# Three-term latent scores in row halves, expert weights addressed by a register, and four of twelve key tiles summed on GpSimd

## The chip, the cores and the metric

The kernel runs on one core of a Trainium2 chip. The metric is the device time of one execution in microseconds (us), as the median of several. The engines of the core are TensorE (PE; its weight loads are PEld), VectorE (DVE), ScalarE (ACT), GpSimd (POOL) and SyncE (SP), which here only issues DMAs. Each engine works through its own queue in order and waits at its head for semaphores that the others raise.

## The reference, cut to what matters

A decoder of two layers on 32 sequences of 56 tokens and 256 channels, each layer with self-attention, cross-attention to a context and a mixture of experts. The change touches the cross-attention of layer 0 and both mixtures. The cross-attention, after its weights are folded into one latent query of 64 numbers per head, is this (B = 32 batches, 16 heads, 56 queries, 1500 keys of 64 numbers):

```python
kv_rope = kv_c * cos[None] + _rotate_half(kv_c) * sin[None]
q_r = jnp.einsum('bshq,hqr->bhsr', q_big, W_qr)
k_r = jnp.einsum('bld,hdr->bhlr', kv_rope, W_kr)
scores = jnp.einsum('bhsr,bhlr->bhsl', q_r, k_r)
attn = jax.nn.softmax(scores, axis=-1)
ctx_c = jnp.einsum('bhsl,bld->bhsd', attn, kv_rope)
```

The mixtures send each token to two experts (of 16 in layer 0, of 7 in layer 1), and add a shared expert:

```python
for e in range(E):
    out = out + combine[:, e:e + 1] * (jax.nn.silu(xf @ w1[e]) @ w2[e])      # layer 0
u = jnp.einsum('nh,ehi->eni', xt, Wup) + bup[:, None, :]                      # layer 1
g = jax.nn.silu(jnp.einsum('eni,eij->enj', u, Wgate) + bgate[:, None, :]) * u
eo = jnp.einsum('enj,ejh->enh', g, Wdown) + bdown[:, None, :]
```

## The kernel before

It is written engine by engine: every stage is a block with one program for each engine, and semaphores order them. The latent cross-attention runs over the 32 batches, two to a turn of a hardware loop (`over_tiles`). `par` is the parity of the batch and picks one of two buffers. The 1500 keys of a batch are KT = 12 tiles of KP = 125 keys. Per batch:

- SP loads the context rows (`raw`), and copies the queries with their two halves of partitions exchanged (`QS`).
- GpSimd rotates the rows: cosine product (L1517), two sine products (L1519, L1522), their sum (L1525), and, when ScalarE has made the f16 high part of the rotated keys (`high`, L1659), the low part (L1531). Keys and queries are pairs of f16 numbers, high and low.
- TensorE transposes high and low parts of a key tile together (`turn`, L1562), eight tiles, then four, each group after the pair of tiles that `TURNS = (5, 9)` names; ScalarE evicts them to `kT` (`evacuate`, L1650).
- TensorE makes the scores of a tile for two groups of eight heads: `QT` (L1606) and then `QS` (L1610) against the same `kT`, which gives all four products of high and low parts. Two tiles make a pair; between pairs it multiplies the exponentials of the pair before with the rows (`values`, L1575).
- ScalarE takes the exponential of a tile (L1682) into one of six buffers `Pb`. A buffer is free when `values` and the sum have read it.
- VectorE sums the twelve tiles of exponentials into `dsum`, one add of 896 columns a tile (first L1742, then L1745), for the softmax denominators.
- After a batch's last tiles, `denominators` (L1585) multiplies `dsum` with ones into PSUM bank 7. VectorE then does four steps in the next batch, one behind each of its adds of tiles 2 to 5 (`attended`): reciprocal (L1718), two checks of its range (L1723, L1726), and the product with the values (L1731), which raises `ct_made`.

The second `turn` writes bank 7, where the denominators of the batch before lie, so it waits for that `ct_made`:

```python
pe.wait_ge(kl_made, b + 1)
if c == 1 and past(b, 2):

    pe.wait_ge(ct_made, b - 1)
```

The mixtures (`experts`) gather tokens into blocks of 256 that belong to one expert: 29 blocks in layer 0 and 20 in layer 1, after 8 blocks of the shared expert. The weights of all experts stand in SBUF (`w2i`, `w2d`; biases `bug`). A table `tab` names the expert of each block. For each block SP loads the number into a register and copies that expert's weights, SBUF to SBUF, into one of three slots (`wbi`, `wbd`, `bugb`); TensorE waits for them (`inward`, `gates` in layer 1, `outward`). SP loads the block's rows too (`xb`). GpSimd scatters the results (L2068).

## Time and profile before

| | |
|---|---|
| median of 3 runs | 2298.38 us (2295.24 to 2302.3) |
| the profiled execution | 2300.62 us, of which 2298.9 us are the span of the records |
| TensorE busy | 1684.6 us, 73% |
| VectorE busy | 1609.3 us, 70% |
| ScalarE busy | 1042.4 us, 45% |
| GpSimd busy | 735.1 us, 32% |

The 1.7 us between the profiled execution and its span lie around the records. The shares are means over the whole span. A row of a timeline gives start and duration in us, the engine, the line of the kernel and what was written from what; a matmul's duration includes its way through the array, so that consecutive ones overlap, and their spacing is the distance of their starts. What stands in brackets at a row's end is how long the engine had been idle and what ended it.

### The profile page before, as it was taken

The numbers are of one execution on the slowest core, as the hardware profiler recorded it, in microseconds if no ns is written. First come the engines' busy times: TensorE is split into PE (matmuls) and PEld (weight loads), VectorE is DVE, ScalarE is ACT, GpSimd is POOL, SyncE is SP. The second block draws the span as 40 slices with busy tenths as digits, with TensorE's granted clock in tenths as the row PEclk, the third lists the DMA queues.
The fourth block names the chain that finished last, engine by engine and source line by source line (L and its number), as shares of the span: only waits on it lengthen the run. The fifth ranks groups of instructions, "written<-read, shape, count | busy, mean of one in ns | idle before, by whom it ended". The sixth has DMA issues, their size and how long they took to land. (4 is left out here: it accounts for less than half of the span.)

```text
span 2298.9 us, 33509 instructions
## 1 busy us (share of the span) xinstructions
PE 1684.6 (73%) x10424; PEld 1020.2 (44%) x10424; DVE 1609.3 (70%) x2595; ACT 1042.4 (45%) x1620; POOL 735.1 (32%) x587
## 2 busy tenths in 40 slices
PE   1444448779999999999977558456776577756883
PEld 0222226434444444444433447434544355534672
DVE  6988882568898898889842833467877465646664
ACT  0433341456666666666621434235555244334452
POOL 1211110024334334433300444323433243436332
PEclk9766665689999999999989679769888699966997
DMA  7800000001101110110000357500000000014465
GB/s 216 262 0 0 0 0 14 7 22 33 32 22 32 32 27 26 32 32 21 25 1 26 94 171 232 188 27 1 0 0 0 25 1 0 0 56 149 153 216 176
DMA packets 88874, 135.17 MB, mean 59 GB/s; under 512 B 14896, under 2 KB 62056, under 8 KB 88378
## 3 DMA queue, kind: packets, MB, share of 16 engines
q1 hardware_dynamic: 81018, 112.89, 16.6%
q0 software_dynamic: 7776, 21.28, 2.5%
q8 instruction: 43, 0.70, 0.1%
q14 instruction: 37, 0.30, 0.0%
HBM read 60.38 MB, written 40.19 MB: 44 GB/s over the span
## 5 line engine op out<-in xcount | busy, mean ns | idle before, releaser
L1682 ACT ACTIVATE lat_Pb<-banks 125x896 f32<-125x896 f32 x384 | 344.7, 916 | 258.9 <-PE banks L1610 221.4
L1745 DVE TENSOR_TENSOR lat_dsum<-lat_dsum,lat_Pb 125x896 f32<-125x896 f32 x320 | 406.9, 1272 | 32.4 <-ACT lat_Pb L1682 26.3
L1575 PE MATMUL banks<-lat_Pb,lat_kv 125*64 125x448 f32 x1536 | 332.3, 554 | 0.0
L1606 PE MATMUL banks<-lat_QT,lat_kT 128*125 (+1 forms) x768 | 279.4, 364 | 7.7 <-ACT lat_Pb L1682 6.3
L1610 PE MATMUL banks<-lat_QS,lat_kT 128*125 128x448 f16 x768 | 272.5, 355 | 0.0
L1531 POOL TENSOR_TENSOR lat_kk<-lat_rot,lat_kk 125x768 f16<-125x768 f32 x32 | 52.5, 1642 | 404.2 <-ACT lat_kk L1659 404.2
L1606 PEld LDWEIGHTS banks<-lat_QT,lat_kT 128*125 128x125 f16 x768 | 105.3, 137 | 130.3 <-issue 66.9
L1575 PEld LDWEIGHTS banks<-lat_Pb,lat_kv 125*64 125x64 f32 x1536 | 93.5, 136 | 153.8 <-issue 109.4
L2068 POOL DMA_INDIRECT sent_outputs<-moe_yb,moe_yidx x98 | 101.5, 1036 | 150.3 <-ACT moe_yb L2297 135.0
L1610 PEld LDWEIGHTS banks<-lat_QS,lat_kT 128*125 128x125 f16 x768 | 106.2, 138 | 30.6
L2464 DVE COPY moe_xTb<-banks 128x1024 f16<-128x1024 f16 x49 | 33.9, 692 | 109.2 <-PE banks L2164 107.1
L1742 DVE TENSOR_TENSOR lat_dsum<-lat_Pb 125x896 f32<-125x896 f32 x32 | 60.8, 1900 | 62.0 <-ACT lat_Pb L1682 62.0
L2120 PE MATMUL banks<-moe_xTb,moe_wbi 128*88 128x256 f16 (+1 forms) x588 | 75.4, 279 | 31.2 <-DMA moe_wbi<-moe_w2i 15.7
L1517 POOL TENSOR_TENSOR lat_rot<-lat_raw,lat_cosK 125x768 f32<-125x768 f32 x32 | 61.0, 1907 | 110.6 <-DMA lat_raw<-in_ctx_dram 110.3
L1718 DVE RECIPROCAL lat_rD<-banks 128x448 f32<-128x448 f32 x32 | 94.3, 2946 | 1.4 <-PE banks L1585 1.4
L2060 POOL DMA_INDIRECT sent_rows<-moe_arena,moe_idx x64 | 73.7, 1151 | 50.8 <-DVE moe_idx L2414 31.7
L622 ACT ACTIVATE causal_WTs<-banks 128x512 f32<-128x512 f32 x64 | 35.1, 595 | 101.8 <-PE banks L667 101.8
L2120 PEld LDWEIGHTS banks<-moe_xTb,moe_wbi 128*88 128x88 f16 (+1 forms) x588 | 60.2, 113 | 44.5 <-DMA moe_wbi<-moe_w2i 21.7
L2198 PE MATMUL banks<-moe_wbd,moe_gT 88*128 88x256 f16 (+1 forms) x588 | 72.2, 272 | 2.5 <-DVE moe_gT L2476 2.5
L749 PE MATMUL banks<-bit_wq,bit_xT 128*128 128x512 f16 x32 | 19.1, 600 | 67.4 <-DVE bit_vf L895 66.9
L392 POOL TENSOR_TENSOR causal_Km<-causal_kT,hmask 128x896 f32<-128x896 f32 x16 | 38.8, 2428 | 81.1 <-ACT causal_qT L543 81.1
L774 PE MATMUL banks<-id,bit_yq 128*128 128x128 f32 x32 | 11.0, 447 | 72.5 <-DVE bit_yq L1016 72.5
(416 smaller groups left out, 3845.8 us busy)
## 6 DMA issues: line engine op xcount, KB each, us to landing
moe_xb<-sent_rows SPq DMA_DIRECT2D x49, 257.0 KB, 3.2
lat_raw<-in_ctx_dram SPq DMA_DIRECT2D x32, 375.0 KB
moe_wbi<-moe_w2i SPq DMA_DIRECT2D x20, 512.0 KB, 3.1
moe_arena<-sent_outputs SPq DMA_DIRECT2D x16, 512.0 KB, 7.0
sent_rows<-zero SPq DMA_DIRECT2D x1, 7453.0 KB, 50.3
lat_QS<-lat_QT SPq DMA_DIRECT2D x64, 112.0 KB, 2.2
sent_rows<-zero SPq DMA_DIRECT2D x1, 5140.0 KB, 68.7
moe_wbd<-moe_w2d SPq DMA_DIRECT2D x20, 256.0 KB
```

The source lines that it names most:

```text
L1517: s(nc.gpsimd.tensor_tensor(rot[:, par], r, cosK[:], ALU.mult))
L1575: ins = nc.tensor.matmul(ps[u * DC:(u + 1) * DC, 4 + par, 0:8 * T], kv[:, par, tt, :], Pb[:, tt % NPB, u, :], start=tt == 0, stop=tt == KT ...
L1606: nc.tensor.matmul(dst, kT[:, par, tt, 0:KP], QT[:, ds(b, 1), heads, :].rearrange("p o h t -> p (o h t)"), start=True, stop=False)
L1610: ins = nc.tensor.matmul(dst, kT[:, par, tt, 0:KP], QS[:, par, heads, :].rearrange("p h t -> p (h t)"), start=False, stop=True)
L1682: nc.scalar.activation(Pb[:, tt % NPB, :, :], ps[0:KP, 2 * (tt % 2):2 * (tt % 2) + 2, 0:8 * T], ACT.Exp, scale=1.0 / QSCALE).then_inc(exp_ ...
L1718: s(nc.vector.reciprocal(rD[:], ps[:, 7, 0:8 * T]))
L1742: ins = nc.vector.tensor_tensor(dsum[:, par], Pb[:, 0], Pb[:, 1], ALU.add)
L1745: ins = nc.vector.tensor_tensor(dsum[:, par], dsum[:, par], Pb[:, tt % NPB], ALU.add)
L2060: nc.gpsimd.indirect_dma_start(xg[:, :], bass.IndirectOffsetOnAxis(ap=idx[:, c, i:i + 1], axis=0), rows[:, i, :], None).then_inc((sent0, s ...
L2068: nc.gpsimd.indirect_dma_start(ytok[:, :], bass.IndirectOffsetOnAxis(ap=yidx[:, n, h:h + 1], axis=0), yb[:, n % 3, h, :], None).then_inc(y ...
L2120: ins = nc.tensor.matmul(ps[0:FP, dst, j * BN:(j + 1) * BN], w[:, u, c, j * FP:(j + 1) * FP], rhs(v, c), start=a + c == 0, stop=a == 2 and ...
L2198: ins = nc.tensor.matmul(dst, gT2[:, n % 2, u, j, h * P:(h + 1) * P], w[:, v, j, :], start=a + j == 0, stop=last and not (gated and b < 0))
```

## The change

There are three parts.

1. Scores. The product of low query and low key parts is left out. `QH` holds the high query parts in both halves of the partitions, `QL` the low ones (four DMAs in place of two). A tile gets a full matmul with `QH` and one with `QL` on only that half of the partitions where its high key parts lie. These alternate from tile to tile (`halves`), and so a pair's four `QL` matmuls come last and alternate between the halves. `TURNS` becomes (7, 9), and ScalarE makes the copies `high` and `rows` behind tiles 4 and 6 instead of 0 and 2.
2. Sums. GpSimd adds tiles 2, 4, 6 and 8 (three adds into `psum`), between its rotation steps, which now run one batch ahead. VectorE adds the other tiles and then `psum`; its four steps `attended` follow its adds of tiles 3, 5, 7 and 9.
3. Experts. TensorE (and ScalarE in layer 1) loads the expert's number into a register and reads the weights where they stand. The copies, their slots and their semaphores go.

```diff
+            def halves(par, low):
+                units = kk[:, par].rearrange("p (a q) u d -> p a (q u) d", q=2)
+                return units[:, :, 1:3, :] if low else units[:, :, 0:4:3, :]
+
+            def paired(a):
+                return a.rearrange("p (a q) d -> p a q d", q=2)
+
             NPB = 6
+            POOLED, NPOOL = (2, 4, 6, 8), 3
+            OWN = (1, 3, 5, 7, 9, 10, None, 11)
+            NSUM, MERGE = len(OWN), 6
+
+            def consumed(b, tt):
+                if tt in POOLED:
+                    return pool_summed, b * NPOOL + max(POOLED.index(tt), 1)
+                return summed, b * NSUM + (OWN.index(max(tt, 1)) + 1)
...
+            psum = sb("psum", [KP, 2, 8 * T], c=main)
...
-            TURNS = (5, 9)
+            TURNS = (7, 9)
...
-                        for half in range(2):
-                            r, o = half * DC, DC - half * DC
-                            sp.dma_start(QS[r:r + DC, par].rearrange("p h t -> p (h t)"),
-                                         QT[o:o + DC, ds(b, 1)].rearrange("p o h t -> p (o h t)")
-                                         ).then_inc(swapped[par], 16)
+                        for half, Q in enumerate((QH, QL)):
+                            for r in (0, DC):
+                                sp.dma_start(Q[r:r + DC, par].rearrange("p h t -> p (h t)"),
+                                             QT[half * DC:half * DC + DC, ds(b, 1)].rearrange(
+                                                 "p o h t -> p (o h t)")
+                                             ).then_inc(spread[par], 16)
...
+                    def add_tile(b, i):
+                        pool.wait_ge(exp_done, b * KT + (POOLED[i + 1] + 1))
+                        if i == 0:
+                            if past(b, 1):
+                                pool.wait_ge(summed, b * NSUM - (NSUM - MERGE - 1))
+                            ins = nc.gpsimd.tensor_tensor(psum[:], Pb[:, POOLED[0] % NPB],
+                                                          Pb[:, POOLED[1] % NPB], ALU.add)
+                        else:
+                            pool.wait_ge(pool_summed, b * NPOOL + i)
+                            ins = nc.gpsimd.tensor_tensor(psum[:], psum[:],
+                                                          Pb[:, POOLED[i + 1] % NPB], ALU.add)
+                        ins.then_inc(pool_summed, 1)
...
+                    def rotate(b, par, step):
+                        r = raw[:, par]
...
+                        if step == 2:
+                            pool.wait_ge(kh_made, b + 1)
+                            if past(b, 2):
+                                pool.wait_ge(kT_done, (b - 1) * NTURN)
+                            nc.gpsimd.tensor_tensor(halves(par, True), paired(rot[:, par]),
+                                                    halves(par, False),
+                                                    ALU.subtract).then_inc(kl_made, 1)
+                            pool.wait_ge(kl_made, b + 1)
...
+                        ahead = live(b + 1, B)
+                        if ahead:
+                            rotate(b + 1, (par + 1) % 2, 0)
+                            rotate(b + 1, (par + 1) % 2, 1)
+                        if live(b, B):
+                            add_tile(b, 0)
+                        if ahead:
+                            rotate(b + 1, (par + 1) % 2, 2)
+                        if live(b, B):
+                            add_tile(b, 1)
+                            add_tile(b, 2)
+
+                    over_tiles(pool, body, 1, s, 3, n=B)
...
                                 for u in range(2):
-                                    heads = slice(8 * u, 8 * u + 8)
-                                    dst = ps[0:KP, 2 * (tt % 2) + u, 0:8 * T]
-                                    nc.tensor.matmul(dst, kT[:, par, tt, 0:KP],
-                                                     QT[:, ds(b, 1), heads, :].rearrange(
-                                                         "p o h t -> p (o h t)"),
+                                    nc.tensor.matmul(ps[0:KP, 2 * (tt % 2) + u, 0:8 * T],
+                                                     kT[:, par, tt, 0:KP], queries(QH, u),
                                                      start=True, stop=False)
-                                    ins = nc.tensor.matmul(dst, kT[:, par, tt, 0:KP],
-                                                           QS[:, par, heads, :].rearrange(
-                                                               "p h t -> p (h t)"),
+
+                            for u in range(2):
+                                for tt in both:
+                                    rows = slice(0, DC) if tt % 2 == 0 else slice(DC, P)
+                                    ins = nc.tensor.matmul(ps[0:KP, 2 * (tt % 2) + u, 0:8 * T],
+                                                           kT[rows, par, tt, 0:KP],
+                                                           queries(QL, u, rows),
                                                            start=False, stop=True)
-                                ins.then_inc(s_done, 1)
+                                    if u == 1:
+                                        ins.then_inc(s_done, 1)
...
-                            if tt == 0 and live(b + 1, B):
+                            if tt == 4 and live(b + 1, B):
                                 high(b + 1, (par + 1) % 2)
-                            if tt == 2 and live(b + 1, B):
+                            if tt == 6 and live(b + 1, B):
...
-                        for tt in range(1, KT):
-                            dve.wait_ge(exp_done, b * KT + (tt + 1))
-                            if tt == 1:
+                        for i, tt in enumerate(OWN):
+                            if tt is None:
+                                dve.wait_ge(pool_summed, (b + 1) * NPOOL)
+                            else:
+                                dve.wait_ge(exp_done, b * KT + (tt + 1))
+                            if i == 0:
                                 if past(b, 2):
 
                                     dve.wait_ge(den_done, b - 1)
                                 ins = nc.vector.tensor_tensor(dsum[:, par], Pb[:, 0], Pb[:, 1], ALU.add)
                             else:
-                                dve.wait_ge(summed, b * (KT - 1) + (tt - 1))
-                                ins = nc.vector.tensor_tensor(dsum[:, par], dsum[:, par],
-                                                              Pb[:, tt % NPB], ALU.add)
+                                dve.wait_ge(summed, b * NSUM + i)
+                                ins = nc.vector.tensor_tensor(
+                                    dsum[:, par], dsum[:, par],
+                                    psum[:] if tt is None else Pb[:, tt % NPB], ALU.add)
                             ins.then_inc(summed, 1)
-                            if tt in range(2, 6) and past(b, 1):
-                                attended(b - 1, (par + 1) % 2, tt - 2)
+                            if i in range(1, 5) and past(b, 1):
+                                attended(b - 1, (par + 1) % 2, i - 1)
...
+                sp.wait_ge(sent0, sent_all)
+                sp.wait_ge(sent1, sent_all)
                 for n in range(NBLK):
-                    s = n % WB
-                    if n >= WB:
-                        load_rows(n + XB - 1)
-                    e = sp.value_load(tab[0:1, n:n + 1], min_val=0, max_val=NR)
-                    if n >= WB:
-                        if gated:
-                            sp.wait_ge(s_made, 2 * (NS + n - WB + 1))
-                        else:
-                            sp.wait_ge(h_done, NS + n - WB + 1)
-                    sp.dma_start(wbi[:, s].rearrange("p u n c f -> p (u n c f)"),
-                                 w2i[:, ds(e, 1)].rearrange("p o u n c f -> p (o u n c f)")
-                                 ).then_inc(wi_in[s], 16)
-                    if gated:
-                        sp.dma_start(bugb[:, s].rearrange("p w j -> p (w j)"),
-                                     bug[:, ds(e, 1)].rearrange("p o w j -> p (o w j)")
-                                     ).then_inc(wi_in[s], 16)
-                    if n >= WB:
-                        sp.wait_ge(y_done, NS + n - WB + 1)
-                    sp.dma_start(wbd[:, s].rearrange("p u c d -> p (u c d)"),
-                                 w2d[:, ds(e, 1)].rearrange("p o u c d -> p (o u c d)")
-                                 ).then_inc(wd_in[s], 16)
-                    if n == WB - 1:
-                        sp.wait_ge(sent0, sent_all)
-                        sp.wait_ge(sent1, sent_all)
-                        for m in range(WB + XB - 1):
-                            load_rows(m)
+                    load_rows(n)
...
+                    if b == 0:
+                        pe.wait_ge(tab_made, 1)
+                        pe.wait_ge(w_split, 2 * NE)
                     if b >= 0:
-                        pe.wait_ge(wi_in[b % WB], per_wi * (b // WB + 1))
+                        expert[b] = pe.value_load(tab[0:1, b:b + 1], min_val=0, max_val=NR)
                         pe.wait_ge(xT_made, b + 1)
                     if n >= 2:
                         pe.wait_ge(u_made if gated else h_made, (2 if gated else 1) * (n - 1))
-                    w = w2i[:, 0, :, 0] if b < 0 else wbi[:, b % WB, :, 0]
+                    w = w2i[:, 0, :, 0] if b < 0 else w2i[:, ds(expert[b], 1), :, 0].rearrange(
+                        "p o u c f -> p (o u) c f")
...
-                    if b >= 0:
-                        pe.wait_ge(wd_in[b % WB], 16 * (b // WB + 1))
...
+                    if b >= 0:
+                        expert[b] = act.value_load(tab[0:1, b:b + 1], min_val=0, max_val=NR)
...
-                    bias = bug[:, 0] if b < 0 else bugb[:, b % WB]
+                    bias = bug[:, 0] if b < 0 else bug[:, ds(expert[b], 1)].rearrange(
+                        "p o w j -> p (o w) j")
```

**On VectorE**, batch 1 of the latent loop. `lat_dsum` is the running sum, `lat_Pb` a tile of exponentials, `lat_rD` the reciprocal, `lat_good` its checks, `lat_QT<-banks,lat_rD` the product that raises `ct_made`. Before:

```order
L1742 TENSOR_TENSOR lat_dsum<-lat_Pb 125x896 [waits lat_exp_done]
L1745 TENSOR_TENSOR lat_dsum<-lat_dsum,lat_Pb 125x896 [waits lat_summed,lat_exp_done]
L1718 RECIPROCAL lat_rD<-banks 128x448 [waits lat_denominators_done]
L1745 TENSOR_TENSOR lat_dsum<-lat_dsum,lat_Pb 125x896 [waits lat_summed,lat_exp_done]
L1723 SCALAR_TENSOR_TENSOR lat_good<-lat_rD,lat_good 128x448 [waits lat_dve]
L1745 TENSOR_TENSOR lat_dsum<-lat_dsum,lat_Pb 125x896 [waits lat_summed,lat_exp_done]
L1726 SCALAR_TENSOR_TENSOR lat_good<-lat_rD,lat_good 128x448 [waits lat_dve]
L1745 TENSOR_TENSOR lat_dsum<-lat_dsum,lat_Pb 125x896 [waits lat_summed,lat_exp_done]
L1731 TENSOR_TENSOR lat_QT<-banks,lat_rD 128x448 [waits lat_pv_done,lat_dve]
L1745 TENSOR_TENSOR lat_dsum<-lat_dsum,lat_Pb 125x896 [waits lat_summed,lat_exp_done] x6
```

The same batch after:

```order
L1801 TENSOR_TENSOR lat_dsum<-lat_Pb 125x896 [waits lat_exp_done]
L1804 TENSOR_TENSOR lat_dsum<-lat_dsum,lat_Pb 125x896 [waits lat_summed,lat_exp_done]
L1774 RECIPROCAL lat_rD<-banks 128x448 [waits lat_denominators_done]
L1804 TENSOR_TENSOR lat_dsum<-lat_dsum,lat_Pb 125x896 [waits lat_summed,lat_exp_done]
L1779 SCALAR_TENSOR_TENSOR lat_good<-lat_rD,lat_good 128x448 [waits lat_dve]
L1804 TENSOR_TENSOR lat_dsum<-lat_dsum,lat_Pb 125x896 [waits lat_summed,lat_exp_done]
L1782 SCALAR_TENSOR_TENSOR lat_good<-lat_rD,lat_good 128x448 [waits lat_dve]
L1804 TENSOR_TENSOR lat_dsum<-lat_dsum,lat_Pb 125x896 [waits lat_summed,lat_exp_done]
L1787 TENSOR_TENSOR lat_QT<-banks,lat_rD 128x448 [waits lat_pv_done,lat_dve]
L1804 TENSOR_TENSOR lat_dsum<-lat_dsum,lat_Pb 125x896 [waits lat_summed,lat_exp_done]
L1804 TENSOR_TENSOR lat_dsum<-lat_dsum,lat_psum 125x896 [waits lat_summed,lat_summed_by_gpsimd]
L1804 TENSOR_TENSOR lat_dsum<-lat_dsum,lat_Pb 125x896 [waits lat_summed,lat_exp_done]
```

The product that raises `ct_made` stood behind the add of tile 5, and stands behind the add of tile 9.

**On GpSimd**, one batch of the same loop. `lat_rot` is the rotated rows, `lat_kk` their high and low parts, `lat_psum` GpSimd's own sum. Before:

```order
L1517 TENSOR_TENSOR lat_rot<-lat_raw,lat_cosK 125x768 [waits lat_odd_rows_loaded,lat_kl_made]
L1519 TENSOR_TENSOR lat_rot<-lat_raw,lat_sinK 125x12x32 [waits lat_pool]
L1522 TENSOR_TENSOR lat_rot<-lat_raw,lat_sinK 125x12x32 [waits lat_pool]
L1525 TENSOR_TENSOR lat_rot<-lat_rot 125x768 [waits lat_pool]
L1531 TENSOR_TENSOR lat_kk<-lat_rot,lat_kk 125x12x64 [waits lat_kh_made,lat_rows_rotated]
```

After:

```order
L1550 TENSOR_TENSOR lat_rot<-lat_raw,lat_cosK 125x768 [waits lat_kv_made,lat_even_rows_loaded]
L1552 TENSOR_TENSOR lat_rot<-lat_raw,lat_sinK 125x12x32 [waits lat_pool]
L1556 TENSOR_TENSOR lat_rot<-lat_raw,lat_sinK 125x12x32 [waits lat_pool]
L1559 TENSOR_TENSOR lat_rot<-lat_rot 125x768 [waits lat_pool]
L1535 TENSOR_TENSOR lat_psum<-lat_Pb 125x896 [waits lat_summed,lat_exp_done,lat_rows_rotated]
L1566 TENSOR_TENSOR lat_kk<-lat_rot,lat_kk 125x6x128 [waits lat_kT_done,lat_kh_made]
L1539 TENSOR_TENSOR lat_psum<-lat_psum,lat_Pb 125x896 [waits lat_summed_by_gpsimd,lat_exp_done,lat_kl_made]
L1539 TENSOR_TENSOR lat_psum<-lat_psum,lat_Pb 125x896 [waits lat_summed_by_gpsimd,lat_exp_done]
```

Three adds of 896 columns are new, one ahead of the low parts of the next batch's keys and two behind them.

**On TensorE**, one routed block of layer 0. Before, its first product:

```order
L2120 MATMUL banks<-moe_xTb,moe_wbi 88x256 [waits moe0_h_made,moe0_block_cols_made,moe0_block_inward_2]
L2120 MATMUL banks<-moe_xTb,moe_wbi 88x256 x11
```

After; `ISA` is a register operation that works out an address:

```order
L2166 TENSOR_LOAD moe_tab
L2166 ISA x2
L2150 ISA [waits moe0_h_made,moe0_block_cols_made]
L2150 MATMUL banks<-moe_xTb,moe_w2i 88x256
L2150 ISA
L2150 MATMUL banks<-moe_xTb,moe_w2i 88x256
L2150 ISA
L2150 MATMUL banks<-moe_xTb,moe_w2i 88x256
L2150 ISA
L2150 MATMUL banks<-moe_xTb,moe_w2i 88x256 x3
```

The wait for a copied weight slot is gone, and a register load with two operations, and one more ahead of most weights, have come.

## Rows read from the trace of the kernel before

**Rows 1.** Windows, 700 to 800 us: PE, PEld, DVE, ACT, POOL busy; clock
```profile
700.00:800.00 100.00, 100.00 (x532) 46.33 (x528) 89.38 (x74) 61.94 (x76) 35.24 (x23) 1.00 0.11 30
```

**Rows 2.** Timeline of TensorE in the latent loop: start, us, operation
```profile
704.30 0.40 PE L1606 MATMUL banks<-lat_QT,lat_kT 128*125 x1
704.54 0.35 PE L1610 MATMUL banks<-lat_QS,lat_kT 128*125 128x448 f16 x1
704.73 0.35 PE L1606 MATMUL banks<-lat_QT,lat_kT 128*125 x1
704.92 0.35 PE L1610 MATMUL banks<-lat_QS,lat_kT 128*125 128x448 f16 x1
...
705.68 0.35 PE L1610 MATMUL banks<-lat_QS,lat_kT 128*125 128x448 f16 x1
705.96 1.72 PE L1575 MATMUL banks<-lat_Pb,lat_kv 125*64 125x448 f32 x8
707.62 0.39 PE L1562 MATMUL banks<-id,lat_kk 125*128 125x125 f16 x4
...
714.33 0.92 PE L1585 MATMUL banks<-lat_dsum,lat_ones 125*64 125x448 f32 x4
```

**Rows 3.** Timeline of ScalarE in the same batch
```profile
702.08 0.92 ACT L1682 ACTIVATE lat_Pb<-banks 125x896 f32<-125x896 f32 x1 [1.92 <-PE banks L1610]
702.89 1.00 ACT L1650 ACTIVATE lat_kT<-banks 128x1000 f16<-128x1000 f16 x1
703.78 0.92 ACT L1682 ACTIVATE lat_Pb<-banks 125x896 f32<-125x896 f32 x1
705.39 1.73 ACT L1682 ACTIVATE lat_Pb<-banks 125x896 f32<-125x896 f32 x2 [0.69 <-PE banks L1610]
...
724.11 1.00 ACT L1650 ACTIVATE lat_kT<-banks 128x1000 f16<-128x1000 f16 x1
```

**Rows 4.** Timeline of VectorE in the same batch
```profile
702.85 0.61 DVE L1723 SCALAR_TENSOR_TENSOR lat_good<-lat_rD,lat_good 128x448 f32<-128x448 f32 x1
...
705.92 0.61 DVE L1731 TENSOR_TENSOR lat_QT<-banks,lat_rD 128x448 f32 x1
706.46 6.71 DVE L1745 TENSOR_TENSOR lat_dsum<-lat_dsum,lat_Pb 125x896 f32<-125x896 f32 x6
...
717.39 2.50 DVE L1745 TENSOR_TENSOR lat_dsum<-lat_dsum,lat_Pb 125x896 f32<-125x896 f32 x1 [0.66 <-ACT lat_Pb L1682]
```

**Rows 5.** Timeline of GpSimd in the same batch
```profile
714.15 1.64 POOL L1531 TENSOR_TENSOR lat_kk<-lat_rot,lat_kk 125x768 f16<-125x768 f32 x1 [12.17 <-ACT lat_kk L1659]
717.11 1.83 POOL L1517 TENSOR_TENSOR lat_rot<-lat_raw,lat_cosK 125x768 f32<-125x768 f32 x1 [1.32 <-DMA lat_raw<-in_ctx_dram]
719.02 1.73 POOL L1519 TENSOR_TENSOR lat_rot<-lat_raw,lat_sinK 125x384 f32<-125x384 f32 x1
...
721.90 1.81 POOL L1525 TENSOR_TENSOR lat_rot<-lat_rot 125x768 f32<-125x768 f32 x1
```

**Rows 6.** VectorE's adds and a GpSimd product by line: duration ns min/median/max
```profile
L1745 DVE TENSOR_TENSOR lat_dsum<-lat_dsum,lat_Pb x320: 1028/1092/2619, 503.3 to 1177.1; 125x896 f32<-125x896 f32 x160
...
L1519 POOL TENSOR_TENSOR lat_rot<-lat_raw,lat_sinK x32: 986/1725/1732, 440.3 to 1121.5; 125x384 f32<-125x384 f32 x32
```

**Rows 7.** Waits in both layers' routed blocks: total us, times, longest
```profile
PE banks L2120 <- DMA moe_wbi<-moe_w2i: 15.7, 17, 2.1
...
PE banks L2120 <- DMA moe_bugb<-moe_bug: 14.9, 8, 3.2
```

**Rows 8.** Register loads by line: SyncE's per block, TensorE's only one
```profile
L1987 SPq TENSOR_LOAD <-moe_tab x49: 264/570/1385, 1332.1 to 2249.0; - x49
...
L1191 PEldq TENSOR_LOAD <-lat_bad x1: 484/484/484, 1186.3 to 1186.3; - x1
```

**Rows 9.** Timeline of TensorE in layer 1's routed blocks
```profile
2182.14 2.45 PE L2120 MATMUL banks<-moe_xTb,moe_wbi 128*128 128x256 f16 x12 [3.25 <-DMA moe_bugb<-moe_bug]
...
2188.18 1.47 PE L2120 MATMUL banks<-moe_xTb,moe_wbi 128*128 128x256 f16 x12
```

84 lines of the change are left out of this document (40 added, 44 removed).

## The prediction

> **What bounds the kernel now.** I read first how busy each engine is by stage, because the whole-span shares (TensorE 73%, VectorE 70%) average over stages with different limits. The latent attention (about 500 to 1180 us) is the longest stage and the one the change rewrites. There TensorE is busy 100.00 of 100 us at a granted clock of 1.00, VectorE 89.38, ScalarE 61.94, GpSimd 35.24 [rows 1]. So TensorE sets the end, and VectorE has a tenth to spare. One batch takes 21.21 us: the same eviction of transposed keys starts at 702.89 and 724.11 [rows 3].
>
> Inside a batch I read TensorE's own timeline. A pair of key tiles takes 707.62 - 704.30 = 3.32 us: eight score matmuls 0.19 apart, then the value products of the pair before [rows 2]. Going from the full-array scores to the half-array values costs 0.28 instead of 0.19, and coming back 0.24 instead of 0.19: 0.15 us per change of array shape. Denominators add 0.75 (their records span 0.92, and a last one's tail of 0.17 lies under what follows), the transposes of the next batch's keys 0.68, which is what is left: 6 x 3.31 + 0.75 + 0.68 = 21.3, near 21.21.
>
> Then I read the timelines of VectorE and GpSimd beside each other, since the change moves work from one to the other. GpSimd's cosine product runs from 717.11 for 1.83, to 718.94. VectorE's add of an exponential tile, which takes 1.08 to 1.12 alone, begins at 717.39 and takes 2.50, to 719.89: it ends 0.95 after GpSimd's end, as if it had not begun before. GpSimd's next product begins at 719.02, when VectorE runs, and takes 1.73 where the shortest of its line takes 0.99: it ends 0.86 after VectorE [rows 4 to 6]. So an add of two SBUF tiles on VectorE and a GpSimd operation run one after the other. VectorE holds the other out for 0.95 us, GpSimd for its duration less the 0.13 (0.99 - 0.86) that it can do while it waits. VectorE's adds have a median of 1092 ns and a maximum of 2619, the product on GpSimd a minimum of 986 and a median of 1725 [rows 6]: this is the rule, not one accident.
>
> In the experts TensorE waits 15.7 us in layer 0 and 14.9 us in layer 1 for the copies of a block's weights [rows 7].
>
> **The change, part by part.**
> *Scores in row halves.* Before: 8 x 0.19 = 1.51 a pair. After: four full matmuls (0.76), one change of shape (0.15), then four on half the rows. If those of different halves run side by side they cost 2 x 0.19: 1.28 in all, and a pair is 1.28 + 0.15 + 1.50 + 0.15 = 3.07. TensorE's own work per batch falls from 21.21 to 6 x 3.07 + 0.75 + 0.68 = 19.85. No row shows row halves; the two halves of the value products, which split the columns, are two f32 streams whose eight records span only 1.72 us, the pace of eight f16 records [rows 2], so I take "side by side"; one after the other would be 0.38 more a pair. The Trainium skill, "TensorE: Matmul & The Clock Gate", in its table of small-K matmuls, states that matmuls in distinct row groups run concurrently; that gives 1.28, and its absence 1.66; no row here shows which.
>
> *When the turn of the next batch's keys may start.* TensorE's second turn (TURNS[1] = 9, in the pair of tiles 8 and 9) overwrites the bank of the denominators and waits for ct_made of the batch before. Before, that multiplication stood behind VectorE's add of tile 5; now it stands behind the add of tile 9, and everything else of that pair must come first. From the last score matmul: 0.47 to the exponential of tile 8 (704.92 to 705.39), 0.81 to the key eviction, 0.89 to the exponential of tile 9, which takes 0.92 [rows 2, 3], 0.12 to VectorE, 1.12 for its add, 0.61 for the multiplication [rows 4]: 4.94. TensorE gets there after 0.19 + 1.80 = 2.0. **It stands still for about 3.0 us per batch, even if nothing else is late.** All of batch b's tiles 10 and 11 are queued behind this turn. With 0.7 us before tile 7, where the copies of rotated keys now stand between exponentials (0.73 each), and some 0.6 elsewhere, a batch would be 19.85 + 3.0 + 1.3 = 24.2.
>
> *GpSimd adds four tiles.* One of its adds is 1.81 for 768 columns [rows 5], so 1.81 x 896/768 = 2.11 for 896, 1.98 of it exclusive. Its work goes from 1.83 + 0.99 + 0.99 + 1.81 + 1.64 = 7.26 to 13.6 us. VectorE loses three adds and keeps eight (8 x 0.95) and two checks of the reciprocal (0.61 less 0.15 each). Together 13.6 + 8.5 = 22.1 us a batch must pass one after the other, against 7.3 + 11.4 = 18.7 before: this alone is over 21.21. In order it is worse, since neither queue can pass its head, and the two alternate. From the end of tile 4's exponential: 0.34 to start, GpSimd's first add 1.98, VectorE's add of tile 5 0.95, GpSimd's subtraction 1.51, check 0.46, GpSimd add 1.98, VectorE tile 7 0.95, GpSimd add 1.98, check 0.46, cosine product for the batch after next 1.65, VectorE tile 9 0.95, gap 0.18, multiplication 0.61 = 14.0. Then TensorE: turn 0.34, pair of tiles 10 and 11 3.07, next batch's first pair with denominators 3.82, second pair 3.07, scores of the third 1.28, a wait of 0.42 for tile 1's scores, and 1.3 to the end of tile 4's exponential. Sum 27.3 us. A walk that starts each operation when its queue, its semaphores and the other engine allow gives 27.2: TensorE then idles 5.7 us at the turn. **27.2 - 21.2 = 6.0 us a batch, over 30 batches 180 us.**
> Of this, 1.0 us a batch hangs on whether the two checks also wait for GpSimd; in no row do they meet it. Both read two SBUF tiles like the adds, so I count them. The Trainium skill, "SBUF — State Buffer", section on its two sides, states it as an exclusive lock for the full instruction, for a VectorE operation with two SBUF inputs; by that they wait (27.2), and without them the batch is 26.2. The adds' rows agree with it (2.50 for 1.08).
>
> *TensorE's clock.* Waits of this length do not occur in this stage now. In the experts, after an idle 3.25 us twelve matmuls took 2.45 instead of 1.47, and 6.04 us went by (2182.14 to 2188.18) for work of 3 x 1.31 + 0.45 = 4.4 [rows 9]. I add 1.7 us to each of 30 batches: 52 us; the bounds are 0 and 60.
>
> *Experts.* The copies go, and with them at most 15.7 + 14.9 = 31 us of waits. Instead TensorE reads the expert's number once a block (49) and computes addresses before 11 or 18 of its matmuls. On SyncE such a load takes 570 ns (its register work I estimate at as much again, from the 264 to 1385 that it spans); the one that TensorE does now took 484 [rows 8]. If it runs while the array still works off the block before, it is free; if not, 49 x 1.0 = 49 us are lost. I take 6 us lost, as TensorE's queue issues ahead of the array, so -25 net; bounds -31 and +18. ScalarE's new load in layer 1 (20 blocks) is hidden by the two products that TensorE does between a block's first and second weights; without that cover it costs up to 20 us. The four spreads of queries instead of two swaps are issued a batch ahead, under the scores of the batch between: nothing; 2 us at the start if not.
>
> **Sum.** 2300.6 (profiled execution) + 180 + 52 - 25 = 2507.6; that execution was 2 us above the median, so 2505 us.
>
> **Rivals.**
> 1. *The checks do not queue behind GpSimd.* 26.2 a batch: +150 + 45 (clock) - 25: 2469.
> 2. *No exclusion that matters, only the late ct_made.* 24.2 a batch, idle 3.0, clock mostly kept: +90 + 30 - 25: 2394. Against it: rows 4 to 6.
> 3. *TensorE's loads are exposed:* 2505 + 43 = 2548.
> 4. *Row halves run one after another* (the change does not do what it says): much falls into the turn's wait; +0.4 a batch, 2517.
> 5. *Faster.* 1.36 x 31 = 42 us of TensorE work and 31 us of waits go, nothing is added: 2226. This decides if ct_made is there when TensorE reaches the turn, within 2.0 us of the last score matmul. For it speaks that TensorE is the bound today; against it the order on VectorE, by which it comes after 4.9 at the earliest.
>
> **How the numbers follow.** Chances: my forecast 0.50, rival 4 0.07, rival 1 0.16, rival 3 0.12, rival 2 0.09, rival 5 0.06. The predicted time is the first. The range goes from rival 2 (2390) to rival 3 with the bounds of the clock and of row halves (2580). A difference under 0.3% can't be told from none here; only a mix of rivals 2 and 5 ends there: faster 0.05, same 0.02, slower 0.93.
>
> **What would show it.** In the changed kernel's trace: a batch of 27 us or more; TensorE idle some 5 us before the transposes of keys in the pair of tiles 8 and 9, released by VectorE's multiplication; VectorE's adds with a median near 2 us; GpSimd's new adds at 2.1 or more; half-row matmuls in twos with equal starts; scores' matmuls slow after the turn; no DMA waits in the experts, blocks near 3.1 us in layer 0 and 4.4 in layer 1. Wrong if VectorE's adds stay near 1.1 while GpSimd adds, or if the turn finds ct_made there.

## The result, and the profile after

The changed kernel takes 2478.2 us (median of 4 runs, 2475.34 to 2481.2) against 2300.34 us for the kernel before on the same chip: ratio 1.0768, 95% interval 1.073 to 1.0807. The forecast was 2505 us, slower. The mechanism can be read off the trace almost step for step; the sizes of three terms were off.

The stretches of the latent stage, as in [rows 1]:

```profile
core 0: us, PE busy (x) PEld busy (x) DVE busy (x) ACT busy (x) POOL busy (x), PEclk, DMA share, GB/s
...
700.00:800.00 100.00, 75.22 (x380) 28.21 (x380) 69.71 (x43) 45.08 (x55) 57.65 (x31) 0.88 0.11 27
```

TensorE was busy 100.00 of 100 us; now it stands still a quarter of the time, at a clock of 0.88. VectorE is less busy too (69.71 for 89.38). No engine is full: a chain of waits sets the pace, and the busy shares do not show which.

TensorE's timeline over one batch (start, duration, engine and line, idle time before it and what ended that), as in [rows 2]:

```profile
start us, us, engine line op out<-in xcount [idle before <-releaser]
...
700.60 0.92 PE L1657 MATMUL banks<-lat_QH,lat_kT 128*125 128x448 f16 x4
701.46 0.59 PE L1664 MATMUL banks<-lat_QL,lat_kT 64*125 64x448 f16 x4
701.98 1.72 PE L1624 MATMUL banks<-lat_Pb,lat_kv 125*64 125x448 f32 x8
709.17 0.58 PE L1611 MATMUL banks<-id,lat_kk 125*128 125x125 f16 x4 [5.46 <-DVE lat_QT L1787]
709.54 1.70 PE L1657 MATMUL banks<-lat_QH,lat_kT 128*125 128x448 f16 x4
...
713.85 1.21 PE L1657 MATMUL banks<-lat_QH,lat_kT 128*125 128x448 f16 x4
...
717.07 0.92 PE L1634 MATMUL banks<-lat_dsum,lat_ones 125*64 125x448 f32 x4
717.93 0.97 PE L1657 MATMUL banks<-lat_QH,lat_kT 128*125 128x448 f16 x4
...
721.00 0.97 PE L1657 MATMUL banks<-lat_QH,lat_kT 128*125 128x448 f16 x4
...
728.80 0.92 PE L1657 MATMUL banks<-lat_QH,lat_kT 128*125 128x448 f16 x4
...
737.36 0.58 PE L1611 MATMUL banks<-id,lat_kk 125*128 125x125 f16 x4 [5.46 <-DVE lat_QT L1787]
...
740.30 2.97 PE L1624 MATMUL banks<-lat_Pb,lat_kv 125*64 125x448 f32 x8
...
746.18 0.92 PE L1634 MATMUL banks<-lat_dsum,lat_ones 125*64 125x448 f32 x4
...
766.47 0.58 PE L1611 MATMUL banks<-id,lat_kk 125*128 125x125 f16 x4 [5.46 <-DVE lat_QT L1787]
```

The first batch shown is 728.80 - 700.60 = 28.20 us. TensorE is idle 5.46 us before the second turn, released by VectorE's multiplication (L1787). And the scores behind that idle take 1.70 instead of 0.92: the pair from 709.54 to 713.85 takes 4.31, an undisturbed one (717.93 to 721.00) 3.07. The granted clock is 0.50 from 709.20 to 711.20 and 1.00 from 717.00 to 721.00: the lower and the upper of its two levels.

Not every batch is like the first. From the second turn at 737.36 to the next at 766.47 it is 29.11 us, and there the value products are slow too (2.97 instead of 1.72). The 27 batches between the second turns at 537.59 and 1310.80 take 28.2 to 29.4 us, 28.6 in the mean, and they differ only in the stretch from the second turn to the denominators, which takes 7.90 to 9.12 us, 8.34 in the mean. At full clock its parts take 0.23 for the turn, 3.03 for the pair behind it (they start at 702.29 and 702.52 in experiment 10, what follows at 705.55) and 2.98 for the pair ahead of the denominators (743.20 to 746.18 here): 6.24. So the slow clock costs 1.7 to 2.9 us a batch, 2.1 in the mean, and without it every batch takes 26.5.

In the first batch, from 701.46, where the first half-row matmul starts, to 701.98, where the first value product starts, is 0.52 us.

VectorE and GpSimd between exponential 4 and the multiplication, as in [rows 4, 5] (the columns of this and every later timeline are those above):

```profile
697.14 1.45 DVE L1804 TENSOR_TENSOR lat_dsum<-lat_dsum,lat_Pb 125x896 f32<-125x896 f32 x1
698.51 2.06 DVE L1779 SCALAR_TENSOR_TENSOR lat_good<-lat_rD,lat_good 128x448 f32<-128x448 f32 x1
700.80 2.66 DVE L1804 TENSOR_TENSOR lat_dsum<-lat_dsum,lat_Pb 125x896 f32<-125x896 f32 x1 [0.22 <-ACT lat_Pb L1738]
703.39 2.49 DVE L1782 SCALAR_TENSOR_TENSOR lat_good<-lat_rD,lat_good 128x448 f32<-128x448 f32 x1
705.81 2.68 DVE L1804 TENSOR_TENSOR lat_dsum<-lat_dsum,lat_Pb 125x896 f32<-125x896 f32 x1
708.41 0.61 DVE L1787 TENSOR_TENSOR lat_QT<-banks,lat_rD 128x448 f32 x1
```

```profile
695.56 2.08 POOL L1535 TENSOR_TENSOR lat_psum<-lat_Pb 125x896 f32<-125x896 f32 x1 [11.69 <-ACT lat_Pb L1738]
697.60 2.50 POOL L1566 TENSOR_TENSOR lat_kk<-lat_rot,lat_kk 125x768 f16<-125x768 f32 x1
700.34 2.17 POOL L1539 TENSOR_TENSOR lat_psum<-lat_psum,lat_Pb 125x896 f32<-125x896 f32 x1 [0.24 <-POOL lat_kk L1566]
703.24 2.16 POOL L1539 TENSOR_TENSOR lat_psum<-lat_psum,lat_Pb 125x896 f32<-125x896 f32 x1 [0.72 <-ACT lat_Pb L1738]
705.36 2.19 POOL L1550 TENSOR_TENSOR lat_rot<-lat_raw,lat_cosK 125x768 f32<-125x768 f32 x1
```

Read the two together. GpSimd's add ends at 702.51, VectorE's add that began at 700.80 ends at 703.46, 0.95 later; the next one ends at 705.40, the check that began at 703.39 at 705.88; the cosine product ends at 707.55, the last add at 708.49, 0.94 later. From 695.56 to 709.02 one of the two is always in an operation: 13.5 us, where the forecast had 14.0 less the 0.34 to start. Both checks of the reciprocal (L1779, L1782) wait in this chain: 2.06 and 2.49 for 0.61. So *the checks queue too*, which rival 1 denied. The Trainium skill, "SBUF — State Buffer", section "SBUF: two separate sides", names the VectorE operation with two SBUF inputs as one that takes the lock against a GpSimd operation that reads SBUF; the checks' rows agree. And GpSimd is idle 11.69 us before its first add: it has time, but not here.

One sign of the prediction did not come. VectorE's adds of a tile (192 of L1804) have a median of 1.23 us, not near 2: of the eight adds of the batch shown only the three above (1.45, 2.66, 2.68) meet a GpSimd operation, and the others take 1.09. GpSimd's own adds take 2.08 to 2.18, as forecast. What counts is which adds are long, and these stand ahead of the multiplication.

In the experts, blocks of layer 0 (first product of each), and the load of the expert's number:

```profile
1586.34 1.47 PE L2150 MATMUL banks<-moe_xTb,moe_w2i 128*88 128x256 f16 x12
...
1589.40 1.48 PE L2150 MATMUL banks<-moe_xTb,moe_w2i 128*88 128x256 f16 x12
```

```profile
engine op xcount: duration ns min/median/max, first and last start us, forms
L2166 PEldq TENSOR_LOAD <-moe_tab x49: 297/306/493, 1569.4 to 2425.3; - x49
L2166 PEldq FUSED_REGOPS  x49: 151/151/165, 1569.8 to 2425.8; - x49
```

Blocks follow each other every 3.07 us in layer 0, and every 4.38 us in layer 1, with no wait for weights and no gap for the load.

### The profile page after: what moved, and what is told of

The parts are those of the page before. It is cut to its first block and busy times, and to the rows that moved or that the text cites. A ratio compares the mean times of both kernels' runs of the same rounds, so it can differ in the third digit from the quotient of the medians.

```text
span 2473.6 us, 34038 instructions
## 1 busy us (share of the span) xinstructions
PE 1701.8 (69%) x10424; PEld 965.6 (39%) x10424; DVE 1639.0 (66%) x2499; ACT 1040.2 (42%) x1620; POOL 970.0 (39%) x683
## 5 line engine op out<-in xcount | busy, mean ns | idle before, releaser
L1804 DVE TENSOR_TENSOR lat_dsum<-lat_dsum,lat_Pb 125x896 f32<-125x896 f32 x192 | 318.9, 1661 | 230.8 <-ACT lat_Pb L1738 229.5
L1657 PE MATMUL banks<-lat_QH,lat_kT 128*125 128x448 f16 x768 | 215.9, 401 | 19.8 <-ACT lat_Pb L1738 17.6
L1535 POOL TENSOR_TENSOR lat_psum<-lat_Pb 125x896 f32<-125x896 f32 x32 | 66.5, 2079 | 366.8 <-ACT lat_Pb L1738 361.8
L1657 PEld LDWEIGHTS banks<-lat_QH,lat_kT 128*125 128x125 f16 x768 | 93.5, 151 | 158.0 <-ACT lat_Pb L1738 127.4
L1539 POOL TENSOR_TENSOR lat_psum<-lat_psum,lat_Pb 125x896 f32<-125x896 f32 x64 | 139.5, 2180 | 30.9 <-ACT lat_Pb L1738 23.8
L1664 PE MATMUL banks<-lat_QL,lat_kT 64*125 64x448 f16 x768 | 127.0, 413 | 0.0
L2232 PE MATMUL banks<-moe_w2d,moe_gT 88*128 (+3 forms) x780 | 103.0, 282 | 17.3 <-DVE moe_gT L2516 13.7
L2232 PEld LDWEIGHTS banks<-moe_w2d,moe_gT 88*128 88x128 f16 (+1 forms) x780 | 76.3, 101 | 32.9 <-issue 22.2
L1782 DVE SCALAR_TENSOR_TENSOR lat_good<-lat_rD,lat_good 128x448 f32<-128x448 f32 x32 | 77.9, 2433 | 0.0
L2150 PE MATMUL banks<-moe_xTb,moe_w2i 128*88 128x256 f16 (+1 forms) x588 | 73.6, 276 | 0.0
```

Of the source, the lines that this page charges most:

```text
L1539: ins = nc.gpsimd.tensor_tensor(psum[:], psum[:], Pb[:, POOLED[i + 1] % NPB], ALU.add)
L1657: nc.tensor.matmul(ps[0:KP, 2 * (tt % 2) + u, 0:8 * T], kT[:, par, tt, 0:KP], queries(QH, u), start=True, stop=False)
L1664: ins = nc.tensor.matmul(ps[0:KP, 2 * (tt % 2) + u, 0:8 * T], kT[rows, par, tt, 0:KP], queries(QL, u, rows), start=False, stop=True)
L1782: s(nc.vector.scalar_tensor_tensor(good[:], rD[:], SAFE, good[:], ALU.is_le, ALU.mult))
L1804: ins = nc.vector.tensor_tensor(dsum[:, par], dsum[:, par], psum[:] if tt is None else Pb[:, tt % NPB], ALU.add)
L2150: ins = nc.tensor.matmul(ps[0:FP, dst, j * BN:(j + 1) * BN], w[:, u, c, j * FP:(j + 1) * FP], rhs(v, c), start=a + c == 0, stop=a == 2 and ...
```

## Experiments

All are compared with the kernel before, which gave 2297.8 to 2301.4 us beside them. Comparisons between them are of medians.

**1. The experts' part alone.** The kernel before with the experts function of the change:

```diff
-                    w = w2i[:, 0, :, 0] if b < 0 else wbi[:, b % WB, :, 0]
+                    w = w2i[:, 0, :, 0] if b < 0 else w2i[:, ds(expert[b], 1), :, 0].rearrange(
+                        "p o u c f -> p (o u) c f")
```

> The kernel before with only the experts' part of the change. My theory (the register loads are hidden, the copies' waits go): blocks 3.07 us apart in layer 0 and 4.38 in layer 1, 37 us less than before, about 2262. Rival (the regular blocks of the changed kernel owe something to the later start or another state of the DMA queues): part of the waits stays, 2275 to 2290. Rival (loads cost): 2300 or more.

2255.55 us, ratio 0.9801 (0.9769 to 0.9834): -44 us. The change holds a part that pays, and it pays more than the 31 us of recorded waits.

**2. Row halves alone.** The kernel before with the row-half scores, every placement as before:

```diff
-            TURNS = (7, 9)
+            TURNS = (5, 9)
-                            if tt == 4 and live(b + 1, B):
+                            if tt == 0 and live(b + 1, B):
                                 high(b + 1, (par + 1) % 2)
-                            if tt == 6 and live(b + 1, B):
+                            if tt == 2 and live(b + 1, B):
```
The lines show it against the changed kernel; beside them VectorE adds all tiles, and the experts are those of the kernel before.

> The kernel before with only the scores in row halves: VectorE adds all twelve tiles, turns at tiles 5 and 9 and the copies behind tiles 0 and 2 as before. If TensorE's own work sets the batch, it falls by 1.36 us to 19.85: 42 us less, 2258. My walk says that it does not: with the low products last in a pair, ScalarE gets both tiles of a pair late and at once, and its copies between two exponentials then hold TensorE up (0.7, 0.8 and 0.4 us a batch), while VectorE has 18 us of its own and meets GpSimd: 21.8 us a batch, 2300 to 2320.

2318.16 us, ratio 1.0079 (1.006 to 1.0099): slower, though TensorE has less to do. Its timeline, and ScalarE's in the same stretch:

```profile
702.47 0.59 PE L1634 MATMUL banks<-lat_QH,lat_kT 128*125 128x448 f16 x2
703.58 0.59 PE L1634 MATMUL banks<-lat_QH,lat_kT 128*125 128x448 f16 x2 [0.52 <-ACT lat_Pb L1715]
```

```profile
701.07 0.92 ACT L1715 ACTIVATE lat_Pb<-banks 125x896 f32<-125x896 f32 x1 [1.37 <-PE banks L1641]
701.88 0.83 ACT L1697 ACTIVATE lat_kv<-lat_rot 125x768 f32<-125x768 f32 x1
702.61 0.91 ACT L1715 ACTIVATE lat_Pb<-banks 125x896 f32<-125x896 f32 x1
704.88 1.73 ACT L1715 ACTIVATE lat_Pb<-banks 125x896 f32<-125x896 f32 x2 [1.35 <-PE banks L1641]
```

A copy (701.88) stands between the two exponentials of a pair, and the next pair's odd tile waits for the second. With row halves both tiles of a pair are released together, at the pair's end, so ScalarE can no longer work the first one off early.

**3. The turn waits for the reciprocal only.** The turn overwrites the denominators' bank, which only the reciprocal reads:

```diff
                             s(nc.vector.reciprocal(rD[:], ps[:, 7, 0:8 * T]))
+                            dve.wait_ge(own, s.at)
+                            dve.sem_inc(den_read, 1)
...
-                            pe.wait_ge(ct_made, b - 1)
+                            pe.wait_ge(den_read, b - 1)
```

> The changed kernel, but the second turn waits only until VectorE's reciprocal has read the denominators' bank, not for the product three steps later. If the late product were the whole cause, the 5.5 us at the turn and the slow clock behind it would go: 21.5 a batch, about 2280. If VectorE and GpSimd, which keep each other out, are the limit beneath, the wait moves to the denominators and to tile 11: my walk gives 26.0 a batch with the clock kept up, about 2410.

2445.11 us, ratio 1.0621 (1.0585 to 1.0656): 33 us back, where 2280 would be 198. The walk's 2410 is missed too; it kept the clock up, and the granted clock from 700 to 800 is 0.92. The stall moved to the next thing that the same chain makes, the sums for the denominators:

```profile
712.03 1.76 PE L1635 MATMUL banks<-lat_dsum,lat_ones 125*64 125x448 f32 x4 [3.87 <-DVE lat_dsum L1807]
```

So the late ct_made alone is not the cause (the rival at 2280 falls); VectorE as a whole is behind.

**4. No GpSimd adds.** The changed kernel, with all adds on VectorE:

```diff
-            OWN = (1, 3, 5, 7, 9, 10, None, 11)
+            OWN = tuple(range(1, KT))
```

> The changed kernel without GpSimd's adds: VectorE adds all twelve tiles and does its four steps behind tiles 2 to 5 as before; row halves, later turns (7, 9), later copies (4, 6) and experts stay. If GpSimd's adds are the whole cause, TensorE is the limit again: 20 to 22 a batch, 2220 to 2285. My walk gives 25.3 plus a slow clock, since GpSimd's rotation then meets VectorE's adds and not the reciprocal: 2380 to 2430.

2348.99 us, ratio 1.0209 (1.0175 to 1.0243), between the two times that were expected. Giving three of VectorE's adds to GpSimd, and with them the multiplication its place behind tile 9 in place of tile 5, cost 2478 - 2349 = 129 us. What is left over the experts alone is 93 us. The trace shows one place: GpSimd works from 696.21 to 706.63 on the subtraction and the next rotation, idle for 0.23 us once, in the very stretch from the reciprocal (693.33) to the multiplication (704.89) in which two of VectorE's adds take 2.70 and 1.88 and its two checks 2.06 and 1.42. The turn waits 2.29 us for that multiplication:

```profile
705.65 0.57 PE L1588 MATMUL banks<-id,lat_kk 125*128 125x125 f16 x4 [2.29 <-DVE lat_QT L1764]
```

**5. The four steps one add earlier.** GpSimd adds as in the change; the multiplication stands behind the add of tile 7:

```diff
-                            if i in range(1, 5) and past(b, 1):
-                                attended(b - 1, (par + 1) % 2, i - 1)
+                            if i in range(0, 4) and past(b, 1):
+                                attended(b - 1, (par + 1) % 2, i)
```

> The changed kernel with one edit: each of VectorE's four steps for the batch before (reciprocal, two range checks, multiplication) stands one add earlier, so that the multiplication which the turn waits for is queued behind the add of tile 7 and not behind that of tile 9. Theory (order on VectorE and the alternation with GpSimd set the batch): by a walk through the queues a batch falls from the measured 28.2 us to about 25 to 26, in all 70 to 110 us less than the changed kernel, 2370 to 2410 us. Rival (the sum of exclusive VectorE and GpSimd work, 22 us, and TensorE's slow clock hold the batch anyway): within 20 us of the changed kernel, 2460 to 2480 us.

2329.82 us, ratio 1.0128 (1.0101 to 1.0156): 148 us back from one place in one queue, where the walk gave 110 at most.

```profile
701.39 0.38 PE L1611 MATMUL banks<-id,lat_kk 125*128 125x125 f16 x4 [0.45 <-DVE lat_QT L1787]
...
709.89 0.97 PE L1634 MATMUL banks<-lat_dsum,lat_ones 125*64 125x448 f32 x4 [1.64 <-DVE lat_dsum L1804]
```

```profile
700.00:800.00 100.00, 87.19 (x474) 30.66 (x470) 85.56 (x52) 56.08 (x70) 74.06 (x34) 1.00 0.13 34
```

(The last row is the stretch 700 to 800, with the columns of the first view above.) The turn waits 0.45 instead of 5.46, and the longest idle time of TensorE's matmuls in this stage is 1.7: the clock stays at 1.00, which I had not counted. The batch is 23.9 us (multiplications at 700.63 and 724.49) against 28.6; of the difference 2.1 us are the slow clock and 2.7 the chain. From the first to the last reciprocal it is 731.9 us for 873.1, which is 141 of the 148.

**6. Half-row matmuls in another order.** Same-half matmuls next to each other in the queue:

```diff
-                            for u in range(2):
-                                for tt in both:
+                            for tt in both:
+                                for u in range(2):
```

> The changed kernel with the four half-row score matmuls of a pair issued tile by tile, so that neighbours use the same half of the rows instead of different halves. Theory (neighbours in different halves run side by side): a pair of QL matmuls can no longer overlap, 0.38 us a pair more; most of it falls into the wait at the turn, so the whole goes up by 0.3 to 0.6 us a batch, 2485 to 2500 us, and the four matmuls span about 0.2 to 0.4 us more in the trace. Rival (they run one after the other already, or the order is without effect): the same time as the changed kernel and the same span of the four.

2475.99 us, ratio 1.0765 (1.0734 to 1.0795): no difference, and not the 2485 to 2500 that was expected. The first half-row matmul and what follows the four are as far apart as in the changed kernel (703.63 to 704.16 is 0.53):

```profile
703.63 0.60 PE L1664 MATMUL banks<-lat_QL,lat_kT 64*125 64x448 f16 x4
704.16 1.72 PE L1624 MATMUL banks<-lat_Pb,lat_kv 125*64 125x448 f32 x8
```

A narrower stretch of the same timeline, 703.6 to 703.8:

```profile
703.63 0.41 PE L1664 MATMUL banks<-lat_QL,lat_kT 64*125 64x448 f16 x2
```

Two matmuls of at most 0.40 span 0.41: they start together. The records of the single matmuls say which two. In this order the second and the fourth of the queue raise the semaphore of their tile; the two that raise none start at 703.634 and 703.641, the two that raise it at 703.874 and 703.881, and so it is in all 192 pairs. So the third of the queue starts ahead of the second, beside the first. Whether the two also share the time, or are worked off one after the other behind records that start together, experiment 7 tells.

**7. All four on one half.** The odd tile's correction then reads the wrong half of the keys; its right correction is left out.

```diff
-                                    rows = slice(0, DC) if tt % 2 == 0 else slice(DC, P)
+                                    rows = slice(0, DC)
```

> The changed kernel, but all four half-row score matmuls of a pair read rows 0 to 63, also for the odd tile (whose correction term then uses the wrong half of the keys: left out of the computation is the odd tiles' right correction). Theory (matmuls in different halves run side by side, and the order of issue does not matter because each half works off its own): now nothing can overlap, the four start 0.19 us apart, and from the first of them to the first value product 0.90 us pass instead of 0.52; the whole stays or grows by up to 12 us, since most of it falls into the wait at the turn. Rival (nothing ran side by side; the records start together but the array works them off in turn): 0.52 us as before.

2515.93 us, ratio 1.0937 (1.0908 to 1.0967).

```profile
707.64 0.97 PE L1664 MATMUL banks<-lat_QL,lat_kT 64*125 64x448 f16 x4
708.53 1.72 PE L1624 MATMUL banks<-lat_Pb,lat_kv 125*64 125x448 f32 x8
```

0.89 us instead of 0.52: now they run one after the other, so in the changed kernel they ran side by side, in either order. Rival 4 falls. The Trainium skill, "TensorE: Matmul & The Clock Gate", section "Why this matters for your kernels", row on small-K matmuls, states that matmuls in distinct row groups are concurrent: the trace agrees. The price, 38 us, is above the 12 that I allowed: I took it for hidden in the wait at the turn. So it is: that wait falls from 5.46 to 3.48 us a batch, against 6 x 0.38 = 2.3 us of longer pairs. What is left is the clock. Behind the shorter wait it stays low for longer; the value products of this batch take 3.25 for 1.72:

```profile
725.38 3.25 PE L1624 MATMUL banks<-lat_Pb,lat_kv 125*64 125x448 f32 x8
```

From the second turn to the denominators 27 batches take 10.66 us in the mean, for 6.99 at full clock (0.23, 3.41 and 3.35): the slow clock costs 3.7 us a batch in place of 2.1, and these 1.6 us over 30 batches are more than the whole price. Why the shorter wait costs more clock is open.

**8. The range checks left out.** The two comparisons of stages 1 and 2 are gone (the range check of the denominators is left out), all else as in the change:

```diff
-                        if stage == 1:
-                            s(nc.vector.scalar_tensor_tensor(good[:], rD[:], 1.0 / SAFE, good[:],
...
-                        if stage == 2:
-                            s(nc.vector.scalar_tensor_tensor(good[:], rD[:], SAFE, good[:],
```

> The changed kernel without the two comparisons of the reciprocals with the safe range on VectorE (the range check of the denominators is left out; the reciprocal and the multiplication stay, each where it was). Theory (both checks queue behind GpSimd's operations in the chain that ends at the turn): 1.0 us a batch for the queueing and some of their own 0.6 go, a batch falls from 28.2 to 26.8 to 27.3, in all 30 to 45 us less than the changed kernel, about 2440 us. Rival (they fill time in which VectorE would wait for the next exponential anyway): within 10 us of the changed kernel.

2414.37 us, ratio 1.0491 (1.0461 to 1.0521): 64 us less, more than the 30 to 45 expected. The wait at the turn fell from 5.46 to 3.24:

```profile
722.31 0.58 PE L1611 MATMUL banks<-id,lat_kk 125*128 125x125 f16 x4 [3.24 <-DVE lat_QT L1780]
722.68 1.70 PE L1657 MATMUL banks<-lat_QH,lat_kT 128*125 128x448 f16 x4
```

VectorE and GpSimd ahead of that turn:

```profile
720.27 1.35 DVE L1797 TENSOR_TENSOR lat_dsum<-lat_dsum,lat_Pb 125x896 f32<-125x896 f32 x1 [1.54 <-ACT lat_Pb L1738]
720.64 2.65 POOL L1550 TENSOR_TENSOR lat_rot<-lat_raw,lat_cosK 125x768 f32<-125x768 f32 x1
```

Without the checks the last add starts ahead of GpSimd's cosine product, and the product waits (2.65 us); with them the product came first (705.36 and 705.81 above) and the add waited. So the chain loses the two checks' 0.5 us each and the product's 1.7, and gains waits for exponentials: from GpSimd's first add to the end of the multiplication it is 11.2 us for 13.5. The expectation had left the order as it was. The slow scores are still there after 3.24 idle.

**9. Row halves with the placement as before.** All adds on VectorE, TURNS (5, 9), copies behind tiles 0 and 2, experts changed (experiment 2's diff, with the experts of experiment 1):

> Changed kernel's row halves and experts, but VectorE adds all tiles, the turns stand behind tiles 5 and 9 and the copies of rotated keys behind tiles 0 and 2 as before. Theory (the parts add up: row halves alone were +18 us, the experts alone -45): 2274 us, within 8; against the kernel with late turns and copies (2349) it puts the late placement at 75 us. Rival (row halves free TensorE, which only pays once the experts no longer wait, or the parts overlap): 2240 or less.

2272.55 us, ratio 0.9877 (0.9849 to 0.9904). The parts add up (2318 - 44 = 2274). Against experiment 4, which differs only in where turns and copies stand, it puts the late placement at 76 us. Between 560 and 1160 us TensorE's matmuls wait 80.6 us in experiment 4 and 31.1 in this one: 45.2 for the multiplication and 23.0 for the sums of exponentials, for which this one does not wait at all. The difference is 2.0 us a batch, about 60 of the 76 us.

**10. Another placement.** What row halves lose is ScalarE work inside a pair; so the evictions of transposed keys and the copy `rows` are moved behind odd tiles, while `high` stays behind tile 0. Against the kernel of experiment 9:

```diff
-            TURNS = (5, 9)
+            TURNS = (4, 8)
-                            if tt == 2 and live(b + 1, B):
+                            if tt == 3 and live(b + 1, B):
```
The edit of experiment 3 comes with it; what each of the two gives alone was not tested.

> Row halves, the changed experts, all adds on VectorE, and another order: the turns stand behind tiles 4 and 8, so that ScalarE evicts the transposed keys behind tiles 5 and 9 (odd ones, whose exponential closes a pair), the copies of rotated keys stand behind tiles 0 and 3, and the second turn waits for the reciprocal alone. Theory (what row halves lost was ScalarE work between the two exponentials of a pair, on which the next pair's scores wait): a walk gives 20.7 us a batch instead of 21.2, 17 us less than the experts alone, about 2238 us, and under the kernel with early turns (2273). Rival (the exponentials alone hold each pair at more than TensorE's 3.07 us, whatever stands between them): 2265 to 2275.

2243.91 us, ratio 0.9757 (0.9729 to 0.9784): the fastest version of this study, 56 us under the kernel before. The batch shown is 20.45 us; batches take 19.9 to 21.7, 20.7 in the mean:

```profile
702.52 0.92 PE L1635 MATMUL banks<-lat_QH,lat_kT 128*125 128x448 f16 x4
...
709.12 0.97 PE L1612 MATMUL banks<-lat_dsum,lat_ones 125*64 125x448 f32 x4 [0.43 <-DVE lat_dsum L1781]
...
722.74 0.39 PE L1589 MATMUL banks<-id,lat_kk 125*128 125x125 f16 x4
722.97 0.36 PE L1635 MATMUL banks<-lat_QH,lat_kT 128*125 128x448 f16 x1
```

TensorE's own work, which the prediction put at 19.85, is nearly all of that.

**11. The same placement without row halves.** The kernel before with the experts of the change and the edits of experiment 10:

> The kernel before with the changed experts and the new order alone (turns behind tiles 4 and 8, copies behind tiles 0 and 3, the second turn waits for the reciprocal), scores in full-array matmuls as before. Theory (TensorE is 100 of 100 us busy in this stage without row halves, so an order that only frees ScalarE and VectorE earlier has nothing to give): 21.2 us a batch, the same as the experts alone, 2255 us within 5; the 12 us that the last version was faster then belong to the row halves. Rival (the order itself saves time): 2245 or less.

2255.27 us, ratio 0.981 (0.9786 to 0.9833), the same as the experts alone, and its interval lies just above that of experiment 10 (0.9786 against 0.9784). The placement has nothing to give while TensorE is full; the 11 us are the row halves'.

## Why the prediction was right, and where its sizes were off

- *The turn waits for a late multiplication.* Right: idle 5.46, forecast 5.7; experiment 5 gave 148 us back by moving it one add.
- *VectorE's two-input operations and GpSimd's exclude each other.* Right in rule and size: chain 13.5 for 13.66, steps of 0.94 to 0.95. The checks queue (rival 1 falls). The forecast priced that queueing at 1.0 us a batch; experiment 8 gave 2.2 us at the turn, but it takes their own time away too and changes the order behind them, so it does not measure that price alone.
- *A batch of 27.2 plus 1.7 for the clock.* Measured 28.6 in the mean, of which 26.5 stand without the slow clock and 2.1 are the clock. So the walk was 0.7 too long (0.4 of it in the chain, which from the end of tile 4's exponential is 13.62 us for 14.0), and the 1.7 taken from [rows 9] 0.4 too little: some -20 and +11 us over 30 batches. That they nearly cancel is luck. From the first to the last reciprocal 651.2 us became 873.1: +221.9 for the stage where the sum had 180 + 52 = 232 (and 1.7 x 30 is 51).
- *Row halves side by side.* Right (experiment 7), and a pair is 3.07 as forecast. Two readings behind that sum are off without changing it: 0.15 is the price of both changes of array shape around the scores (0.09 and 0.05), not of each, and the other 0.15 of a pair lies in the value products (705.96 to 707.62 is 1.66); and what is left of 21.21 for the transposes is 0.60, not 0.68.
- *Experts -25.* The term most off: from ScalarE's first eviction of a routed block to its last, the two stretches fell from 104.7 to 84.8 and from 100.4 to 80.8 us, -39.5. The loads of the expert's number cost nothing (306 ns each, under the array's work), so the 6 us that I put down for them were not lost; rival 3 falls. And the waits cost more than their 30.6 us [rows 7]: the idle time of a row counts from the modelled end of the matmul before, but the next block would have started earlier than that. Two blocks of layer 0 in the kernel before (TensorE's timeline):

```profile
1381.40 1.51 PE L2120 MATMUL banks<-moe_xTb,moe_wbi 128*88 128x256 f16 x12 [0.32 <-DMA moe_wbi<-moe_w2i]
...
1385.75 1.51 PE L2120 MATMUL banks<-moe_xTb,moe_wbi 128*88 128x256 f16 x12 [1.07 <-DMA moe_wbi<-moe_w2i]
```

  A wait recorded as 1.07 put the second block 4.35 us behind the first, 1.28 more than 3.07. For the 25 waits that is 5 of the missing 9 us. Another 3 are slow clock, which the sum priced in the attention and forgot here: behind waits of 3.25 and 2.71 two blocks of layer 1 took 6.04 (2182.14 to 2188.18 [rows 9]) and 6.05 us (2216.18 to 2222.23) for 4.38.
- *The other rivals.* Rival 2 (no exclusion, 2394) falls by the rows of VectorE and GpSimd above, rival 5 (faster) by the wait of 5.46.
- The rest of the span gives -7.7, 222 - 39.5 - 7.7 = 175 (the spans are 2298.9 and 2473.6) against 180 + 52 - 25 = 207 forecast. Of the 7.7, 5.7 lie before the first reciprocal of the loop; their cause is open.

What a single price means here: against the experts alone (2256), early row halves cost 17 us, their late placement 76, GpSimd's adds 129. But these are not prices of the parts. GpSimd's adds with the multiplication one add earlier are 19 us faster than no adds at all in the late placement (2330 and 2349). Why the late placement costs 76 us without GpSimd's adds was read from the traces (experiments 4 and 9) and not tested by itself.
